# Post-norm decoder layer: the last two groups become a chunk each, and the last attention step takes eight quads of experts

## The reference

```python
x = _layernorm(x + attn_ref(x, ...))        # RMS norms, causal conv of 3 taps, minGRU scan, 128->512->128 GELU MLP
x = _layernorm(x + xattn_ref(x, ctx, ...))  # 16 heads of 64 over 120 context rows, causal mask, softmax
x = _layernorm(x + ffn_ref(x, ...))         # shared expert + top 2 of 16 experts (128 -> 64 -> 128)
# the experts' part of ffn_ref:
router_logits = jax.nn.sigmoid(x @ gate_w + gate_b)
expert_values, expert_indices = jax.lax.top_k(router_logits, k=TOP_K)
expert_values = expert_values / jnp.sum(expert_values, axis=-1, keepdims=True)
# ... all experts are computed, two are selected per token and weighted
return x + _mlp(x, shared_wg, shared_wu, shared_wd) + expert_weighted
```

## Time and profile before

| | |
|---|---|
| median of 3 runs | 1594.81 us (1594.42 to 1595.85) |
| the profiled execution | 1600.01 us, span 1598.3 us, mean granted clock 0.947 |
| attention of group 15 ends (last x2) | 1472.18 us |
| slots of chunk 7 written | 1486.70 us |
| last expert output copied | 1549.64 us |
| last output store issued | 1594.83 us |

### The profile page before, as it was taken

How to read it: one execution, slowest core, us unless ns; L and a number is a source line. 1 busy time by engine, 2 the same in 40 slices (tenths; PEclk the granted TensorE clock), 3 DMA queues, 4 the chain that set the end, 5 groups by cost and what they waited for, 6 DMA issues and landing times. The chain is left out here.

```text
span 1598.3 us, 34208 instructions
## 1 busy us (share of the span) xinstructions
PE 1325.3 (83%) x11168; PEld 1077.9 (67%) x11168; DVE 1021.7 (64%) x2723; ACT 877.6 (55%) x3239; POOL 835.5 (52%) x996
## 2 busy tenths in 40 slices
PE   2889797989898997989888998989889898986650
PEld 1667676777776776767667776767667776865540
DVE  3566657566656777666776767667776767666233
ACT  3656555475655665575665655575665656553120
POOL 4353435553446546663566545664566545564344
PEclk9999998999999999999999999999999999998575
DMA  6000000032112212132122212133122222133651
GB/s 209 8 7 8 7 8 14 12 99 71 38 55 69 83 57 59 47 110 78 36 63 83 84 50 64 45 101 90 33 65 75 82 60 64 36 91 103 178 158 46
DMA packets 142896, 105.78 MB, mean 66 GB/s; under 512 B 12352, under 2 KB 137856, under 8 KB 142720
## 3 DMA queue, kind: packets, MB, share of 16 engines
q1 hardware_dynamic: 132224, 84.71, 18.4%
q0 software_dynamic: 8192, 16.79, 3.7%
q10 hardware_dynamic: 2304, 2.10, 0.5%
HBM read 69.99 MB, written 33.55 MB: 65 GB/s over the span
## 5 line engine op out<-in xcount | busy, mean ns | idle before, releaser
L1593 POOL TENSOR_TENSOR pr<-pr,ri 128x480 f32<-128x480 f32 x256 | 250.8, 993 | 274.1 <-DVE ri L1227 272.2
L918 ACT ACTIVATE pr<-sE,nm 128x120 f32<-128x120 f32 x512 | 178.0, 360 | 249.4 <-DVE nm L1213 249.3
L918 ACT ACTIVATE pr<-sO,nm 128x120 f32<-128x120 f32 x512 | 179.4, 383 | 0.0
L590 PE MATMUL pvb<-pT,vv 120*64 120x128 f32 x2048 | 142.9, 283 | 43.4 <-DVE pT L1223 43.0
L557 PEld LDWEIGHTS sE<-kT,qT 64*128 64x128 f32 x1024 | 126.4, 191 | 55.0 <-issue 55.0
L1633 POOL DMA_INDIRECT gat<-sorted_y,slot x128 | 127.9, 999 | 65.2 <-issue 47.4
L590 PEld LDWEIGHTS pvb<-pT,vv 120*64 120x64 f32 x2048 | 112.2, 139 | 73.1 <-DVE pT L1223 56.7
L1621 POOL DMA_INDIRECT sorted_x<-x,slot x128 | 128.2, 1002 | 48.9 <-issue 34.5
L557 PE MATMUL sE<-kT,qT 64*128 64x120 f32 x1024 | 150.2, 288 | 0.0
L557 PE MATMUL sO<-kT,qT 64*128 64x120 f32 x1024 | 150.2, 288 | 0.0
L416 PE MATMUL t<-ident_f,pr 128*120 128x128 f32 x1024 | 145.3, 288 | 2.4 <-POOL pr L1593 2.0
(11 more groups left out here) (333 smaller groups left out, 3533.6 us busy)
## 6 DMA issues: line engine op xcount, KB each, us to landing
wq<-in_w_e SPq DMA_DIRECT2D x224, 128.0 KB
sorted_y<-yq SPq DMA_DIRECT2D x64, 256.0 KB, 2.5
xq<-sorted_x SPq DMA_DIRECT2D x56, 256.0 KB, 2.8
xt<-in_x SPq DMA_DIRECT2D x16, 256.0 KB, 3.0
sorted_x<-yq SPq DMA_DIRECT2D x16, 256.0 KB, 4.1
out_y<-y SPq DMA_DIRECT2D x64, 64.0 KB, 1.6
cT<-in_ctxT SPq DMA_DIRECT2D x16, 240.0 KB, 3.1
sorted_x<-x,slot POOLq DMA_INDIRECT x128
```

Of the source, the lines that this page charges most:

```text
L590: ins = mm(pvb[r * DK:(r + 1) * DK, (k // 2) * T:(k // 2 + 1) * T], vv[:, q, h * DK:(h + 1) * DK], pT[:, 4 * r + k // 2, :], start=True, s ...
L918: ins = f(pr[:, p % RING, r, i, :], score_banks[r][:, i * S:(i + 1) * S], ACT.Exp, bias=nm[:, p % 2, r, i:i + 1], accum_out=rsum[:, p % 2, ...
L1593: GP.tensor_tensor(pr[:, p % RING, r, :, :], pr[:, p % RING, r, :, :], ri[:, p % 2, r, :, :].to_broadcast([P, 4, S]), ALU.mult).then_inc(s ...
```

## The change

The two last groups, 14 and 15, become a chunk each (chunks 7 and 8) of 24 tiles or 6 quads. Their quads are `LAST` .. `LAST+5` and `LAST+6` .. `LAST+11`. `body` for t = 16 is gone.

- At t = 15 the experts of chunk 6 are all done: eight quads, one in every s from 2 to 9 (`up_in`). POOL also scatters chunk 7 there (s = 3 to 6, two each), DVE works out its slots at s = 1, and SP loads the weights of the first four quads of chunk 7 at s = 4 to 7 and their x at s = 8.
- Behind the pipeline the router of group 15, its slots and its 8 scatters are woven between the six quads of chunk 7; then the six quads of chunk 8 follow. PSUM banks alternate over t0/pvb, t1/ma and sE/sO.
- The sums of groups 12 to 15 have buffers of their own for all four sequences (`gat_last`, `ys_last`, `y_last`, statistics in cT), are taken a group at a time, and the deviation is made once per group (`e_ln4`). `sorted_y` has three buffers instead of two.

```diff
+LONE_TILES = 24
+DEEP = G // 2 - 2
+LONE = G // 2 - 1
+LAST = LONE * TILES // QUAD
+TAIL = G - 4
...
-            for t in range(-1, G + 1):
-                if t < G - 1:
-                    body(there(t + 1), there(t), there(t - 1), there(t - 3), [there(t - 5)] if t >= 5 else [])
-                elif t == G - 1:
-                    body(None, t, t - 1, t - 3, [t - 5, t - 4])
-                else:
-                    body(None, None, t - 1, t - 3, [])
+            for t in range(-1, G - 1):
+                body(there(t + 1), there(t), there(t - 1), there(t - 3), [there(t - 5)] if t >= 5 else [])
+            body(None, G - 1, G - 2, G - 4, [G - 6, G - 5])
+
+        def up_in(d, s):
+            if d is None:
+                return None
+            if d == G - 4:
+                return QUADS * d + s - 2 if 2 <= s < 2 + 2 * QUADS else None
+            return QUADS * d + s // 2 - 1 if s % 2 == 0 and 2 <= s <= 2 * QUADS else None
...  # SP, the last attention step
+                if d == G - 4:
+                    n = QUADS * d
+                    for s in range(2, PAIRS + LAG + 1):
+                        for e, q in sums_in(es, s - 1):
+                            e_store(e, q)
+                        if n + s < LAST:
+                            x_load(n + s)
+                        if s > 2:
+                            if n + s - 1 < LAST:
+                                w_load(n + s - 1)
+                            d_store(n + s - 3)
+                        if s == 4:
+                            sp.wait_ge(sem["a_bank"], whole("a_bank", G - 1))
+                        if 4 <= s < 8:
+                            w_load(LAST + s - 4)
...  # PE, in each s of a step (ACT and DVE alike)
-                    if D and s > 1 and odd:
-                        d_down(QUADS * d + (s - 3) // 2)
-                    if D and s > 1 and not odd:
-                        d_up(QUADS * d + s // 2 - 1, c)
+                    if up_in(d, s - 1) is not None:
+                        d_down(up_in(d, s - 1))
+                    if up_in(d, s) is not None:
+                        d_up(up_in(d, s), c if s == 2 else None)
...  # ACT, behind the pipeline
+            d_tanh(LAST + 3)
+            w_load(END - 3)
+            for n in range(LAST + 4, END + 2):
...
+                elif n < LAST + LONE_QUADS:
+                    d_y(n - 2)
+                    d_tanh(n)
+                    w_load(END - 2 + n - LAST - 4)
...  # DVE, behind the pipeline
+            d_act(LAST + 5)
+            for i in range(3):
+                d_act(n + i)
+            e_sums(TAIL + 1)
+            d_act(n + 3)
+            e_ln3s(TAIL + 1)
+            d_act(n + 4)
+            d_act(n + 5)
+            for e in (TAIL + 2, TAIL + 3):
+                e_sums(e)
+                e_ln3s(e)
```

More of the change, by code:

```diff
@@ L191, in layer_kernel @@
         wide = 2 * I + P
[L192 to L195, removed]
-        hq_last = gin[:, 0:2 * P].rearrange("p (v n) -> p v n", v=2)
+        half = QUAD * P
@@ new lines, in layer_kernel @@
+        x_last = [xt[:], xm[:], xg[:], xz[:], xq[0][:], xq[1][:]] + \
+            [carve(flat(kT), 2 * QUAD * wide + half * i, P) for i in range(3)] + \
+            [carve(flat(hT), half * i, P) for i in range(2)] + [carve(flat(xc), 0, P)]
+        hq_last = gin[:, 0:2 * P].rearrange("p (v n) -> p v n", v=2)
+        spent = pr[:].rearrange("p k r i s -> p (k r i s)")
+        gat_last = [spent[:, half * i:half * i + half].rearrange("p (q m n) -> p q m n", q=2, m=2) for i in range(4)]
+        ys_last = [x1[:], cv[:]]
@@ L198, in last, with deep @@
+        y_last = [carve(flat(wo), half * i, P) for i in range(2)]
+        st_last = cT[:, 0:12 * SEQ].rearrange("p (r q n) -> p r q n", r=2, q=SEQ)
+        mv_last = cT[:, 12 * SEQ:16 * SEQ].rearrange("p (r q n) -> p r q n", r=2, q=SEQ)
+        ve_last = cT[:, 16 * SEQ:18 * SEQ].rearrange("p (r q) -> p r q", r=2)
+        rs_last = cT[:, 18 * SEQ:20 * SEQ].rearrange("p (r q) -> p r q", r=2)
         def last(n):
             return n >= LAST
+        def deep(n):
+            return quads_before(DEEP) <= n < LAST
@@ L314, in w_load @@
             def w_load(n):
-                k = n // quads
-                if n % quads == 0 or last(n):
+                k = chunk_at(n)
+                if n == quads_before(k) or last(n):
                     sp.wait_ge(sem["expert"], upto("expert", k))
@@ L364, in body @@
                         w_load(QUADS * d + i)
[L365 to L379, removed]
+                if d == G - 4:
[13 more added lines that the diff above has]
+                            w_load(LAST + s - 4)
+                        if s == 8:
+                            sp.wait_ge(sem["ln1_out"], whole("ln1_out", G - 1))
+                            for i in range(4):
+                                x_load(LAST + i)
                     return
@@ L781, in _ @@
             pipeline(body)
-            for i in range(quads + 2):
-                if i < quads:
-                    d_T(LAST + i)
-                if 0 < i <= quads:
-                    d_up(LAST + i - 1)
-                if i > 1:
-                    d_down(LAST + i - 2)
+            c = G - 1
+            d_down(LAST - 1)
+            d_T(LAST)
+            d_T(LAST + 1)
+            c_x2_T(c)
+            d_up(LAST)
+            c_router_shared(c)
+            d_up(LAST + 1)
+            d_down(LAST)
+            c_shared_T(c)
+            d_T(LAST + 2)
+            d_up(LAST + 2)
+            d_T(LAST + 3)
+            c_rank(LONE + 1)
+            c_shared_down(c)
+            d_down(LAST + 1)
+            d_up(LAST + 3)
+            for n in range(LAST + 4, END + 2):
+                if n == LAST + LONE_QUADS:
+                    d_down(n - 2)
+                    d_down(n - 1)
+                if n < END:
+                    d_T(n)
+                if n > LAST + LONE_QUADS:
+                    if n <= END:
+                        d_up(n - 1)
+                    if n > LAST + LONE_QUADS + 1:
+                        d_down(n - 2)
+                elif n < LAST + LONE_QUADS:
+                    d_down(n - 2)
+                    d_up(n)
         @block.scalar
```

420 lines of the change are left out of this document (267 added, 153 removed).

## The result

The changed kernel took 1606.53 us (median of 5, 1602.79 to 1609.08) against 1595.10 us (1594.42 to 1596.81) of the kernel before: ratio 1.0061, 95% interval 1.0036 to 1.0085. A second comparison, with 10 and 27 runs, gave 1602.91 against 1597.57, ratio 1.0035, interval 1.0014 to 1.0056. The forecast was 1599 us, slower by 3.8. Medians are of all executions; the ratios leave out five, among all kernels here, that ran far longer than their like (1634 to 6884 us).

The account below looks back on a forecast made before the run. No engine was full in the last attention step, a round trip, and the tail was a chain. Attention +33.9, clock +2 and tail -32.1 gave +3.8 on 1594.8, say 1599 us; own range 1593 to 1605, wider 1582 to 1609.

Parts of the forecast that it names:

- Slots and first added quad: Start of last attention step: chunk 7's slots on DVE add 2.4 us, one more quad's `d_up` and gate add 1.6.
- The loop: Last attention step: SP's store waits for y ahead of the next weights; six turns of 12.0 us, +31.5 us.
- the 2 us for the clock: Last attention step: 2 us added in all because PE idles in the loop and its clock may fall.
- Last y to last x2: End of last attention step: last product with V already ahead of y, about 4.5 us instead of 6.1, -1.6.
- Tail: Last x2 to the end: 94 us instead of 126.1, -32.1, with 90 to 98 as bounds.
- ACT is the late one, not the scatters: Tail: ACT's three weight loads, 4.3 us each, delay the first x copy of chunk 8 to T + 43.1.
- no idle of POOL except for sums: Sign in the tail, after chunk 8's `xqT`: POOL idles only for sums, 41 us from third gate to end.
- What was carried over: Whole kernel: the +3.8 us on the profiled span of 1598.3 was added to the median, 1594.8, giving 1598.6.
- A: Faster rival, last attention step: SP loop does not close, +9 to +13 us instead of +31.5, 1577 us; chance 0.18.
- B: Faster rival, tail: PE stays at full clock, fed by chunk 7, 87 us instead of 94, 1591 us; chance 0.17.
- C: Slower rival, last attention step: PE falls to half clock, 13.7 us a turn, 1608 us; chance 0.14.
- D: Rival: the change does not do what it says, a quad of chunk 6 is left for the tail; chance 0.01.

Follow-up runs that it names:

- the kernel with both cuts: Changed kernel with SP's output store behind the loads and DVE's y ahead of its copy of the heads: 1653.40 us, ratio 1.0032 to the kernel before.
- the one with the store behind: Changed kernel with SP's output store moved behind the x load, weight loads and y store of the same s: 1584.49 us, ratio 0.9902 to the kernel before.

## Why the prediction came out as it did

Direction and mechanism were right. The median of the second comparison, 1602.9, lies in the forecast's own range of 1593 to 1605; that of the first, 1606.5, lies above it and inside the wider one, 1582 to 1609. The size was short, +3.8 against +8.0 in the stretches that the change touches and +5 to +11 by medians.

- **Slots and first added quad.** Said +2.4 and +1.6; the first y comes 24.1 us behind the first x load in place of 20.1: +4.0.
- **The loop.** Said 12.0 us a turn at full clock, 13.7 at half, and 2 us in all for the clock: 74. Measured 75.3. The six turns are 12.92, 12.84, 11.14, 12.81, 13.05 and 12.52; the third is the only one whose `d_up` took 1.09 us. So a turn is 11.1 at full clock and 12.8 at half. The difference, 1.7, is the 1.76 of the prediction's bound at half clock. Both ends were 0.9 too long, for two reasons among others: DVE's operations overlap at their ends (from the copy of the heads to y 1.52 us between starts, worked out as 1.82), and the weights are waited for 1.8 us behind the last issue, not 2.06. The mis-sized term is the 2 us for the clock: five turns of six were at half clock, 8.5 us, and 5.2 of them were covered by the loop worked out too long. So it is luck that 74 came so near to 75.3. The rule from the Trainium skill (DMA: Bandwidth & Descriptors, "Issuing engines are not separate DMA queues") that issue time is usually small beside the transfer would have had the turn at 8.7; this trace disagrees, with 3.64 us for four issues and 2.0 to 2.8 from an issue's start to its landing.
- **Last y to last x2.** Said -1.6. From the last of the turns' y it was 6.4 us before (4.8 when repeated) and 5.4 after: -1.0, or +0.6.
- **Where the last x2 came.** Said 1506.1, or 1508.1 with the 2 us for the clock; the profile has 1505.95. That is luck: in this profile the step took 1.9 us more than said, and it began 4.1 earlier than in the profile of before.
- **Tail.** Said 126.1 less 32.1. Measured 95.0 and 95.6. With T for the last x2, slots came at T + 22 (said 20), the third gate at T + 53.6 (52.7), the sums of group 13 ended at T + 59.6 (57.9), and from the third gate to the end it took 41.3 (41). Here the step that failed is a cause: "ACT is the late one, not the scatters". Without ACT's loads the x of chunk 8 was copied 0.6 us earlier, no more. Its first x loads, said to have landed near T + 40, were waited for until T + 44.9, and until T + 44.0 without ACT's loads. ACT's issues, SP's queue with its y stores, and the landing of the x loads end together. What held the gathers of group 14 until 1558.75 (8.98 us of idle) was the landing of chunk 7's last y, which I had not priced: the sign "no idle of POOL except for sums" did not come. It cost nothing, since the last of these four gathers ended at 1563.44 and DVE's sums of group 13 at 1565.58.
- **What was carried over.** I put the difference on the median of before. The profiles' starts of the last step moved by up to 7 us for reasons of their own, and this is as large as the effect.

Of the rivals, A was wrong (no turn of the changed kernel is below 11.0; its price was also a little low, since six turns of 8.5 to 9.0 are 10.5 to 13.5 more than 40.5, not 9 to 13). B was wrong: 95, not 87, and PE did not keep the full clock (1.00 from 1516 to 1526, 0.50 from 1536 to 1546). C was right in what it said of the clock, and in its 1.7 us a turn; its 13.7 was not reached. D did not come about: eight `d_up` from `wq` stand in the step, one in each s from 2 to 9.

## What to carry to other kernels

When a stage gets twice the work, follow each queue's order around once: an issue queue that waits for this step's output ahead of the next step's input closes a loop whose length no engine's busy share shows. A store nobody waits for goes behind the loads. And count the queue's own issues as an engine's work: with the loop open, eight loads of 0.9 us, their address reads, an x load and two stores bound the turn at 10.3 us.

## What the runs showed of the hardware

Landing was slow where the DMA engines were full. In the twelve microseconds from 1540 to 1552 of the changed kernel the DMA engines were nearly full (tenths in 40 slices), and what landed then took 4.8 to 7.4 us; over the whole kernel y stores take 2.5 and x loads 2.8. No run varies this alone, so that the one causes the other is argued, not shown.

```profile
DMA  7488767988778979997998879999999999999999
...
sorted_y<-yq SPq DMA_DIRECT2D x3, 256.0 KB, 5.0
kT<-sorted_x SPq DMA_DIRECT2D x3, 256.0 KB, 4.8
...
xc<-sorted_x SPq DMA_DIRECT2D x1, 256.0 KB, 7.4
```

PE's clock fell to its lower level (0.50) in the middle of attention, behind stretches in which the loop left PE 0.67 and 0.21 us of work in 3, and was the full one again at 1452, with PE working without a gap in between. In the third turn it stayed up (1.00 from 1452 to 1464). It costs 1.7 us of a turn of 12.8.

The same program can cost 50 us more on another occasion: the kernel before took 1597.6 and 1597.4 in two sets of runs and 1647.4 and 1647.7 in the next two. In the traces of the latter, the pipeline steps from about 670 us on take 96 and 91 us by turns (from one load of `xt` to the next) where they took 90 to 92 each before, and the engines stand idle for 1 to 8 us where no wait is shown. What causes this, and why the kernel with both cuts took 69 us more than the one with the store behind, where the kernel before lost 50, stays open.
